# Latent attention: where VectorE weighs the probabilities in its hand-written order

## The reference

```
q      = latent queries of the head, folded to the key width (128)
kv     = rope(ctx[b])                      # 257 keys x 128
prob   = softmax(q @ kv.T)                 # 16 heads x 32 positions = 512 rows, 257 keys
ctx_c  = prob @ kv                         # 512 rows x 128
out   += (ctx_c @ w_kc_kv.T) @ Wo.T        # summed over the 16 heads
```

## Time and profile before

| | us |
|---|---|
| median of 3 runs | 2147.24 (2146.89 to 2147.83) |
| the profiled execution | 2146.89 |
| its span, first to last instruction | 2145.1 |
| mean granted clock of PE | 0.981 |
| PE busy | 2035.0 (95%) |
| DVE busy | 1163.7 (54%) |
| ACT busy | 798.7 (37%) |
| POOL busy | 955.7 (45%) |

### The profile page before, as it was taken

How to read it: one execution, slowest core, us unless ns; L and a number is a source line. 1 busy time by engine, 2 the same in 40 slices (tenths; PEclk the granted TensorE clock), 3 DMA queues, 4 the chain that set the end, 5 groups by cost and what they waited for, 6 DMA issues and landing times. The chain is left out here.

```text
span 2145.1 us, 27878 instructions
## 1 busy us (share of the span) xinstructions
PE 2035.0 (95%) x8746; PEld 1371.8 (64%) x8746; DVE 1163.7 (54%) x2698; ACT 798.7 (37%) x1986; POOL 955.7 (45%) x929
## 2 busy tenths in 40 slices
PE   7999999998999999999998999999978999999995
PEld 6867676686588744666656676667654555555552
DVE  4258888366561122555547788759863434444442
ACT  2354443143411200333335434335524444445441
POOL 1265573211252100577768656366303444555552
PEclk9999999999999999999999999999987999999998
DMA  5220011300211100111122000110344999888886
GB/s 195 99 80 23 23 28 39 80 2 1 100 58 53 34 1 0 32 50 41 55 88 63 25 21 25 63 67 1 104 150 138 307 301 327 211 215 210 215 208 167
DMA packets 83391, 209.19 MB, mean 98 GB/s; under 512 B 13728, under 2 KB 39840, under 8 KB 74752
## 3 DMA queue, kind: packets, MB, share of 16 engines
q1 hardware_dynamic: 60528, 153.54, 20.8%
q0 software_dynamic: 21280, 51.38, 11.7%
q10 hardware_dynamic: 1440, 2.49, 0.3%
HBM read 257.95 MB, written 34.36 MB: 136 GB/s over the span
## 5 line engine op out<-in xcount | busy, mean ns | idle before, releaser
L98 PE MATMUL banks<-L1f_w,L1f_xT 128*128 x760 | 265.3, 492 | 2.6 <-issue 1.3
L2673 POOL DMA_INDIRECT moe_sums<-L1f_y,L1f_row x95 | 150.6, 1585 | 221.6 <-DVE L1f_is_who L2542 150.6
L159 POOL TENSOR_TENSOR rstd<-rstd,power 128x1 f32<-128x1 f32 x48 | 28.6, 596 | 399.3 <-DVE rstd L153 399.3
L98 PEld LDWEIGHTS banks<-L1f_w,L1f_xT 128*128 128x128 f32 x760 | 138.0, 192 | 83.1 <-issue 7.8
L2681 POOL DMA_INDIRECT L1f_xg<-moe_rows,L1f_row x95 | 94.2, 991 | 64.8 <-DVE L1f_row L2537 37.7
L2509 DVE SCALAR_TENSOR_TENSOR L1f_z<-banks,L1f_share,L1f_sg 128x192 f32<-128x192 f32 x95 | 39.7, 418 | 148.5 <-ACT L1f_sg L2444 148.4
L461 PE MATMUL banks<-L0x_wn,L0x_qT 128*128 128x512 f32 x256 | 115.1, 593 | 0.8 <-DVE x L531 0.8
L461 PE MATMUL banks<-L1x_wn,L1x_qT 128*128 128x512 f32 x256 | 115.1, 593 | 0.8 <-DVE x L531 0.8
L98 PE MATMUL banks<-L0f_down,L0f_z 128*128 128x512 f32 x256 | 111.1, 592 | 1.5 <-DVE L0f_z L2000 1.5
L2444 ACT ACTIVATE L1f_sg<-banks 128x192 f32<-128x192 f32 x95 | 31.4, 330 | 206.9 <-PE banks L98 206.9
L98 PE MATMUL banks<-L0f_hT_hi,L0f_ug_hi 128*128 128x512 f32 x256 | 100.0, 391 | 0.0
(11 more groups left out here) (402 smaller groups left out, 5258.5 us busy)
## 6 DMA issues: line engine op xcount, KB each, us to landing
L1f_w<-in_experts SPq DMA_DIRECT2D x95, 1280.0 KB
L1f_laid<-moe_counts SPq DMA_DIRECT2D x59, 512.0 KB, 5.4
w<-in_L1x_heads SPq DMA_DIRECT2D x16, 704.0 KB, 4.0
w<-in_L0x_heads SPq DMA_DIRECT2D x8, 1216.0 KB, 5.2
w<-in_wug SPq DMA_DIRECT2D x8, 1024.0 KB, 4.8
L0x_craw<-in_ctx SPq DMA_DIRECT2D x96, 64.0 KB, 2.1
L1x_craw<-in_ctx SPq DMA_DIRECT2D x96, 64.0 KB, 2.0
w<-in_L0x_out SPq DMA_DIRECT2D x4, 1280.0 KB, 5.6
```

Source lines behind the costliest of these rows:

```text
L98: ins = pe.e.matmul(out, w, m, start=first and n == 0, stop=last and n == len(pairs) - 1)
L159: pool.e.tensor_tensor(self.rstd[:, i:i + 1], self.rstd[:, i:i + 1], self.power[:, 0:1], ALU.pow).then_inc(self.rstd_set.sem, 1)
L2673: pool.e.indirect_dma_start(self.sums[j % 2][:, :], bass.IndirectOffsetOnAxis(ap=self.row[:, j:j + 1], axis=0), self.y[j % self.NY][:], No ...
```

## The change

In DVE's loop, `weigh` is called for batch b at the end of iteration b's work on batches b-3 and b-2, where before it was called for batch b-1 right behind `find_peak(b)`. Nothing is added or removed; the instructions, their operands and the other engines' programs are the same. The buffers still rotate safely, since every wait is kept.

```
--- before.py
+++ after.py
@@ -510,8 +510,6 @@
         for b in range(B + self.LAG_VALUES + BPT):
             if b < B:
                 self.find_peak(dve, b)
-            if 0 <= b - 1 < B:
-                self.weigh(dve, b - 1)
             v, t = b - self.LAG_VALUES, b - self.LAG_TURN
             if 0 <= v < B:
                 dve.wait_ge(self.mixed, v + 1)
@@ -522,6 +520,8 @@
                     hi, lo = cut(self.pT[t % 2], slice(None), c)
                     dve.wait_ge(self.pT_hi, 2 * t + c + 1)
                     dve.e.tensor_tensor(lo, self.t_bank[:, c * BANK:(c + 1) * BANK], hi, ALU.subtract).then_inc(self.pT_lo.sem, 1)
+            if b < B:
+                self.weigh(dve, b)
             o = b - self.LAG_VALUES - BPT
             if o == self.LAST:
                 self.after.halves_lo(dve)
```

## The result

The changed kernel took 2166.85 us (median, 2164.72 to 2169.77) against 2147.06 us for the kernel before: a ratio of 1.0093, 95% interval 1.0082 to 1.0104, so 17.6 to 22.3 us slower, 20.0 in the middle. The prediction said 2166 us, range 2157 to 2188. The profiled execution took 2163.64 us with a span of 2161.8.

A forecast was written before the change was run, and what follows sets the result against it. PE bounds the steady part, the loop DVE, ACT, PE the fills. 8.0 + 7.5 + 2 x 1.0 + 2 x 0.5 = 18.5 us on the span 2145.1, plus 1.8 and 0.35: 2165.7, said as 2166 us; range 2157 to 2188.

The forecast's parts named there:

- the fills: Start of the loops in L0x and L1x: mix(4) starts later, 8.0 us lost in L0x and 7.5 in L1x.
- the rest of the loops: Steady part of both stages: PE stalls some 0.5 us once per stage, 2 x 0.5 us in the sum.
- the clock: Both fills: PE waits, so at least one spell at the lower clock; 1 us per stage, 2 x 1.0 in the sum.
- The ring: DVE's chain per iteration closes: peak(b), exponent(b), pT_hi(b-2), pT_lo(b-2), weigh(b), peak(b+1); 7.28 us in the fill.
- The size of a round: One round in the fill: 1.51 + 3.02 + 1.20 + short weigh 1.55 = 7.28 us, against 6.27 before.
- The short weigh: In the fill rounds POOL is idle again when the next weigh runs, so weigh takes 1.55 us.
- my long one: A weigh beside busy POOL, 3.18 us; taken for the first weigh of L0x and the first two of L1x.
- the upper bound of 4 us per stage: Clock loss if spells at the lower clock last over half of each fill: about 4 us per stage.
- The steady part: DVE's ring averages 8.04 us, just under PE's 8.26, so PE's own work still sets the period.
- The stall of 0.5 us: PE waits for POOL's late keys behind a long weigh, likely only at the first tile: some 0.5 us once per stage.
- Full blocking: Shared port rule taken strictly: each of weigh's four L554 could queue behind a POOL instruction; not used in the sum.
- The third rival: Each L554 waits for one POOL instruction: weigh 5.05 us, +118 us, some 2280 us in all; chance 0.02.

The follow-up runs named there:

- the run with weigh at once: DVE calls weigh(b) right behind peak(b), ahead of ctx and pT_lo, where the kernel before had weigh(b-1) there: ratio 1.0313 to the kernel before, 67 us slower.
- the experiment with the new place and the old batch: Against the kernel before, weigh moves behind pT_lo but still weighs batch b-1: ratio 1.0070, 15.0 us slower.
- the last version: Kernel before with ACT's keep_folded and pT_hi copies ahead of exponent, and DVE changing over to weigh(b) behind pT_lo at batch 3: ratio 0.9991, median 2142.85 us.

## Why the prediction was right

The mechanism was right, and the time came out at 20.0 us for 18.5. That the two are so close is in part luck: against the parts in the trace the fills were put 3.4 us too low (15.5 for 18.9) and the rest of the loops 0.9 too low (1.0 for 1.9), and the clock 2.0 too high. Step by step:

- **The ring.** Predicted: peak, exponent, pT_hi, pT_lo, weigh, each waiting for the one before. Shown by the waits of DVE (seven for pT_hi, two for the exponentials), and by two experiments that open it at one place each: with the wait for the batch's own exponentials gone, rounds stay at 7.4 to 7.5 us; with pT_hi out of it they fall to 6.3. The forecast of 1.8 us of wait ahead of pT_lo was 2.00.
- **The place of the loss.** Predicted: the fills, 15.5 us, 17.5 with the clock. Measured in the profile: 18.9. The change in the fill alone costs as much as the whole within the noise, the rest alone 1.5 to 5.8 us.
- **The size of a round.** 7.28 us predicted, 7.49 measured. The term that was too small is peak: I took 1.51 us from a row with a short L544 (0.17 us). It is 0.17 us in the first round here too, while POOL waits, and that round took 148.41 - 141.20 = 7.21. From the next on `mix` has released POOL just ahead of L544, which takes 0.34 to 0.50 us (0.49 at 157.10). So peak is 157.63 - 155.78 = 1.85 us there; pT_hi and pT_lo are the 3.02 and 1.20 predicted, weigh is 148.41 - 146.95 = 1.46, and a round takes 7.53. The first of the four took 7.37: 7.37 + 3 x 7.53 = 29.96 against 4 x 7.28 = 29.12, 0.84 us per stage.
- **The short weigh.** Right for the fills: L554 x4 took 1.14 us in every round from peak(2) on, with POOL idle. The first one of L0x was longer than my long one, 136.16 - 132.10 = 4.06 us for 3.18, since L549 alone took 0.99 us: another 0.9 us. In L1x the first took 3.83 us and the L544 of peak(1) 0.98, while the second weigh took 2.40 for 3.18: together 0.7 us more than predicted. These sizes make up for what the next step gave too much.
- **The clock.** Right that it falls, wrong in the term of 1 us per stage. PE waited 3.4 us in L0x and was at a mean granted clock of 0.94 in that fill (1.00 before), at 0.51 from 137.6 to 144.5 us. But the round that starts at 141.20, inside that spell, took 7.21 us, no more than the 7.28 predicted without the clock, and `mix(0)` started at 147.13, 0.09 us behind the end of pT_lo. PE had room. The reading behind the term was incomplete too: of the 10 us at the low clock in the fill of L1x before, 6.8 (1133.2 to 1140.0) begin where PE had waited 3.3 us for POOL's first keys, ahead of the first exponential, and the changed kernel has them as well; 3.4 us came behind the wait of 2.0 us that I named. What a spell may do to POOL, and so to DVE, was read in the trace of another kernel and wasn't in my sum, and the upper bound of 4 us per stage had no working beside it.
- **The steady part.** Right that PE stays the bound: busy 193.89 of 194.00 us. The stall of 0.5 us through POOL's keys came too, but not at the first tile, where weigh(10) was short. In L0x it came at the third, behind a short weigh: POOL had the statistics at 277.91, 9.52 us later than before (268.39), while `mix(4)` was only 7.62 us later, a delay of 1.9 us against 1.57 us of slack. The steady part lost 0.47 and 0.3 us, near the 0.5 predicted. Wrong was to leave out the drain, with 0.57 and 0.55 us.
- **Full blocking.** The third rival had each L554 queue behind a POOL instruction, 5.05 us per weigh. The longest weigh was 4.06 us here and 4.07 in the run with weigh at once (3.89 in the round shown): it is neither the short price nor that one. A single instruction does wait as long as that (the first point of the last section), but the four L554 of one weigh took 3.33 us together at most in the changed kernel, where four such waits would be 4.64.

## What to carry to other kernels

In a loop that several in-order engines run with lags, a step moved one iteration earlier can close an engine's chain on itself within one iteration. Add up the closed rings, through every engine's own order, and hold each against the period of the bound engine. Where the bound engine had the longer period the ring was nearly free here (1.0 and 0.9 us per stage); where it hadn't full work yet, in the fill, the difference was paid in each round, 1.2 us by four rounds plus 5 us of first waits, twice (a little less in L1x). And the neighbour's order is part of the ring: with ACT's pT_hi copies ahead of the exponentials the same move cost 6.4 us instead of 20.

## What the runs showed of the hardware

- A VectorE instruction on 128x4 elements took 0.17 us with GpSimd idle and up to 0.99 us beside it (L544 at 1176.15 in the experiment with the new place and the old batch, just behind the start of POOL's L368 at 1176.12); L549, 128x4 with two SBUF inputs, took 0.15 and 0.99 us in the changed kernel (146.95 and 132.10). Both long ones end within 0.03 us of the POOL instruction beside them, an L368 of 0.99 us (1176.12) and one of 1.00 us (132.07). So in these rows a tiny instruction on a critical ring waits for the whole of its neighbour's. The Trainium skill (SBUF — State Buffer, "Who interferes with whom") names both kinds, `tensor_scalar` in a 2-port mode and instructions with two SBUF inputs beside a GpSimd read, as those that contend for the shared pair; the trace agrees.
- The granted clock of PE was at 1.2 GHz from 137.6 to 144.5 us in the fill of the changed kernel, around the end (138.75) of a wait of 3.4 us; in the later rounds of that fill, with a wait of 1.61 us in each, it stayed at 2.4 GHz. The profiled execution of the kernel before had a slower stretch near 24 to 37 us (0.74) that the changed one, with the same instructions there, had not. Two profiles differ by some 2 us for that alone.
- In the last version's comparison the kernel before itself ranged from 2140.8 to 2148.2 us over 27 executions, 0.34%, so a difference of 2 us needs many executions.
